# The last attention of an eight-layer block in half-batch sets: scores on four row tiles, one tiled stretch a set

## The reference, cut to what matters

```python
q = _heads(jnp.concatenate([ssm_states, hidden_states], axis=-1) @ Wq, H)      # 32 heads
kcat = jnp.concatenate([rep(ssm_k), rep(k)], axis=2)                           # 8 heads, each for 4 of q
vcat = jnp.concatenate([rep(ssm_v), rep(v)], axis=2)
scores = jnp.einsum('bhqd,bhkd->bhqk', q, k) / np.sqrt(D)
scores = scores + bias                                                         # a slope per head
scores = jnp.where(mask, scores, -jnp.inf)      # the last 64 states, the last 32 tokens
wei = jax.nn.softmax(scores, axis=-1)
o = jnp.einsum('bhqk,bhkd->bhqd', wei, v)
x = x + o.reshape(B, T, HID) @ Wo
```

## Time and profile before

| | |
|---|---|
| three runs | 2078.51, 2068.67, 2076.16 us (median 2076.16) |
| profiled execution, first to last instruction (no other time of it is given) | 2074.5 us |
| PE busy, whole span | 1853.4 us (89%) |
| DVE, ACT, POOL busy | 1266.8, 1026.9, 730.7 us |
| the changed stage | 1707 to 1954 us of the span |

### The profile page before, as it was taken

One profiled execution on the slowest core, in us unless ns is written; L12 is line 12 of the kernel. 1 busy time (PEld: TensorE's weight loads), 2 busy tenths in 40 slices (PEclk: granted clock), 3 DMA queues, 4 the chain that ended last, 5 costly groups with the idle time before them and its releaser, 6 DMA issues. The chain is left out here.

```text
span 2074.5 us, 42486 instructions
## 1 busy us (share of the span) xinstructions
PE 1853.4 (89%) x12207; PEld 1251.6 (60%) x12216; DVE 1266.8 (61%) x4137; ACT 1026.9 (50%) x2698; POOL 730.7 (35%) x707
## 2 busy tenths in 40 slices
PE   7999999998999888878999989969978799999755
PEld 4677777775565566545666766735545557777533
DVE  6666666665777344656343334368979545656698
ACT  5555555553333443312444434348879524444586
POOL 3333333331000202566455555533300106676410
PEclk9999999999999898979999999989999898999998
DMA  8990000000000000253777776510010111211100
GB/s 305 283 274 1 0 0 0 0 1 0 0 0 0 1 1 33 76 197 120 170 162 169 169 155 136 92 59 2 2 64 1 64 43 26 42 39 36 43 18 24
DMA packets 145607, 145.55 MB, mean 70 GB/s; under 512 B 49376, under 2 KB 133568, under 8 KB 145344
## 3 DMA queue, kind: packets, MB, share of 16 engines
q1 hardware_dynamic: 122432, 113.81, 19.5%
q0 software_dynamic: 23040, 30.01, 8.2%
HBM read 137.12 MB, written 66.44 MB: 98 GB/s over the span
## 5 line engine op out<-in xcount | busy, mean ns | idle before, releaser
L1709 POOL DMA_INDIRECT expert_sums<-moe_rows_in,moe_to x128 | 198.2, 1549 | 158.7 <-DMA expert_sums<-moe_rows_in,moe_to 91.9
L1782 PE MATMUL moe_gate<-moe_places,moe_xt 128*128 x512 | 175.3, 465 | 3.4 <-issue 1.9
L3329 DVE CUSTOM_DVE_ANT_0 ctxt<-wa_score,early 128x128 f32<-128x128 f32 x512 | 114.2, 286 | 101.3 <-PE wa_score L3179 101.3
L1975 DVE COPY moe_ht_e<-moe_turned 128x256 f32<-128x256 f32 x128 | 54.4, 425 | 193.9 <-PE moe_turned L1790 192.5
L570 ACT ACTIVATE ga_prob<-ga_score,ga_neg_max 128x128 f32<-128x128 f32 x256 | 99.6, 390 | 125.7 <-DVE ga_neg_max L443 125.7
L3141 POOL TENSOR_TENSOR ctxt<-ctxt,wa_top 128x512 f32<-128x512 f32 x128 | 131.6, 1040 | 75.4 <-DVE wa_top L3329 75.4
L2065 POOL TENSOR_TENSOR ln_rstd<-ln_var,half 128x4 f32<-128x4 f32 (+1 forms) x16 | 21.5, 1346 | 362.1 <-DVE ln_var L2061 362.1
L190 POOL TENSOR_TENSOR ga_q_inv<-ga_q_sum,half 128x4 f32<-128x4 f32 x64 | 64.4, 1007 | 224.3 <-DVE ga_q_sum L426 224.3
L3278 ACT ACTIVATE wa_pt<-wa_turned 128x512 f32<-128x512 f32 x128 | 76.5, 598 | 129.7 <-PE wa_turned L3188 129.7
L325 PE MATMUL ga_summed<-ga_wo,ga_out_t 128*128 128x256 f32 x512 | 121.2, 380 | 0.7 <-ACT ga_out_t L578 0.7
L1782 PEld LDWEIGHTS moe_gate<-moe_places,moe_xt 128*128 128x128 f32 x512 | 90.5, 189 | 47.2 <-issue 12.1
(11 more groups left out here) (491 smaller groups left out, 4777.6 us busy)
## 6 DMA issues: line engine op xcount, KB each, us to landing
moe_places<-in_L_ffn_packed SPq DMA_DIRECT2D x128, 608.0 KB
slot_x<-zeros SPq DMA_DIRECT2D x24, 1076.0 KB, 16.3
moe_rows_in<-slot_x SPq DMA_DIRECT2D x128, 134.5 KB, 3.0
wa_v<-v_ctx SPq DMA_DIRECT2D x16, 180.0 KB, 3.1
early<-in_L_xattn_Wq SPq DMA_DIRECT2D x5, 512.0 KB, 7.8
x<-in_x SPq DMA_DIRECT2D x4, 512.0 KB, 9.6
ga_wo<-in_L_xattn_Wo SPq DMA_DIRECT2D x1, 2048.0 KB, 15.1
expert_sums<-zeros SPq DMA_DIRECT2D x2, 1024.0 KB, 8.4
```

The lines of the kernel that those rows point to most:

```text
L1709: pool.indirect_dma_start(out=mem.sums[j % SUMS], out_offset=bass.IndirectOffsetOnAxis(ap=to[:, j:j + 1], axis=0), in_=y[:, j, :], in_offs ...
L1782: last = pe.matmul(both[j % 2][:, 0:2 * FE], xt[:, j % 2, c, :], packed[:, place, c * 2 * FE:(c + 1) * 2 * FE].rearrange("p a n -> p (a n) ...
L3329: ins = dve.tensor_tensor_reduce(unit[:, x, :], score[k % 3][:, x * P:(x + 1) * P], w.table[:, k, x, :], 1.0, NEVER, ALU.add, ALU.max, top ...
```

## The change

A set is now half a batch: 4 units, each with a bank of its own (`score` has four banks instead of three), so all four groups of heads, on all four row tiles, are scored in one block of 16 matmuls. Right behind it come the two mixes of earlier sets (the second half of set s-2, the first of s-1). Then all work on the whole array stands together: turning or projecting a batch, four units of turns (the last two of set s-1, the first two of set s), turning back set s-2. To make room, the batch's turn and projection share the bank of `turn_back` (`od` is a part of `back`). ACT copies mixes in two halves; DVE's add stands before the fourth unit of an even set; POOL spreads queries once a set, before its four subtractions. The loops, SP's too, are written out, and the semaphores start without credits.

```diff
-        score = [bank(f"score{j}") for j in range(3)]
+        score = [bank(f"score{r}") for r in range(R)]
...
-        mix_t, back, od = bank("mix_t"), bank("back"), bank("od")
+        mix_t, back = bank("mix_t"), bank("back")
+        od = back[:, 0:H]
...
+                def scores(s):
+                    b, u = divmod(s, 2)
+                    if u == 0 and b >= 1:
+                        pe.wait_ge(made.sem, made.at(HC * b - 1))
+                        pe.wait_ge(keyed.sem, keyed.at(2 * b - 1))
+                    behind(pe, biased, s * R - 1)
+                    for x in range(X):
+                        for r in range(R):
...
+                            last = pe.matmul(score[r][:, x * P:(x + 1) * P], w.qd[rows, b % 2, X * u + x, :], w.keys[rows, b % 2, X * u + x, :],
...
+                def turn_probs(n):
+                    pe.wait_ge(lowered.sem, lowered.at(n))
+                    behind(pe, pt_moved, n - 2)
...
+                def tiled(s):
+                    if s < SETS:
+                        scores(s)
+                    if s >= 2:
+                        pe.wait_ge(mt_moved.sem, mt_moved.at(2 * (s - 2)))
+                        mix_up(s - 2, 1)
+                    if 1 <= s <= SETS:
+                        mix_up(s - 1, 0)
+
+                def whole(s):
+                    if s >= 5:
+                        pe.wait_ge(chain.sem, chain.at(2 * (s - 3) + 1))
+                    if turning(s) >= 0:
+                        turn_mixed(turning(s))
+                    if summing(s) >= 0:
+                        go_down(summing(s))
+                    for n in range(s * R - 2, s * R + 2):
+                        if 0 <= n < SETS * R:
+                            turn_probs(n)
+                    if s >= 2:
+                        behind(pe, chain, 2 * (s - 3) + 1)
+                        behind(pe, o_moved, turning(s))
+                        behind(pe, added, summing(s))
+                        turn_back(s - 2)
+
+                for s in range(SETS + 2):
+                    tiled(s)
+                    whole(s)
+                pe.wait_ge(chain.sem, chain.at(2 * (SETS - 1) + 1))
+                go_down(B - 2)
...
+                for s in range(SETS + 2):
+                    if s >= 2:
+                        move_mixed(s - 2, 1, 2 * (s - 1) if s <= SETS else 2 * (s - 2) + 1)
+                    if 1 <= s <= SETS:
+                        move_mixed(s - 1, 0, 2 * (s - 1))
+                    for n in range(s * R - 2, s * R + 2):
+                        if 0 <= n < SETS * R:
+                            exp(n)
+                        if n == s * R - 2 and turning(s) >= 0:
+                            move_out(turning(s))
+                    if s % 2 == 0 and s + 2 < SETS:
+                        move_keys(s // 2 + 1)
```

More of the change, by code:

```diff
@@ L3143, in batch @@
[L3143 to L3162, removed]
+                def spread(b, c):
+                    behind(pool, scored, (2 * b - 3) * R + R - 1)
+                    spread_queries(pool, w, c, w.q[:, c, b * S:(b + 1) * S], b % 2).then_inc(made.sem, 1)
+                def lower(n):
+                    pool.wait_ge(biased.sem, biased.at(n))
+                    unit = low[:, n % LOWS, :, :]
+                    pool.tensor_tensor(unit, unit, top[:, n % LOWS, :].unsqueeze(2).to_broadcast([P, X, P]), ALU.subtract).then_inc(lowered.sem, 1)
@@ L3164, in _ @@
+                for s in range(SETS):
+                    if s + 2 < SETS:
+                        spread(s // 2 + 1, s % 2)
+                    for r in range(R):
+                        lower(s * R + r)
+                    if s == SETS - 3:
+                        norm.root(pool, 0, 0, LASTG)
             @block.tensor
             def _(pe):
[L3166 to L3176, removed]
+                def scores(s):
[5 more added lines that the diff above has]
+                    for x in range(X):
+                        for r in range(R):
@@ L3182, in scores @@
                                 last.then_inc(scored.sem, 1)
[L3184 to L3188, removed]
+                def turn_probs(n):
+                    pe.wait_ge(lowered.sem, lowered.at(n))
+                    behind(pe, pt_moved, n - 2)
+                    for x in range(X):
+                        last = pe.transpose(turned[n % 2][:, x * P:(x + 1) * P], low[:, n % LOWS, x, :], mem.ident[:, :])
@@ L3203, in mix_up, with turn_back @@
                             last = pe.matmul(mix_t[32 * k:32 * k + 32, x * P + kv_half * 64:x * P + kv_half * 64 + 64],
-                                             v[:, j % 2, QUAD * u + x, head * WD1:head * WD1 + 32], columns[:, :, k, :], start=True, stop=True)
+                                             v[:, b % 2, X * u + x, head * WD1:head * WD1 + 32], columns[:, :, k, :], start=True, stop=True)
                     last.then_inc(mixed_s.sem, 1)
[L3207 to L3211, removed]
+                def turn_back(s):
+                    pe.wait_ge(mt_moved.sem, mt_moved.at(2 * s + 1))
+                    for x in range(X):
+                        last = pe.transpose(back[:, x * P:(x + 1) * P], mt[:, s % 2, x, :, :].rearrange("p k n -> p (k n)"), mem.ident[:, :])
@@ L3219, in turn_mixed, with go_down @@
                     last.then_inc(turn_o.sem, 1)
[L3221 to L3222 removed]
+                def go_down(b):
+                    pe.wait_ge(o_moved.sem, o_moved.at(b))
                     for c in range(HC):
[L3224 removed]
+                        last = pe.matmul(od[:, :], ot[:, c, :], w.wo[:, c, :], start=(c == 0), stop=(c == HC - 1))
@@ L3225, in go_down @@
                     last.then_inc(downed.sem, 1)
[L3227 to L3242, removed]
-                        if k == 6:
-                            turn_back(t, j, 0)
-                        if k == 7 and before >= 1:
-                            turn_mixed(t, j - 1)
@@ L3352, in batch @@
-                def batch(t, j, before=2, final=False):
-                    for k in range(U):
-                        if k < U - LEAD:
-                            lower(t, j, k + LEAD)
-                        elif not final:
-                            lower(t, j + 1, k + LEAD - U)
-                        if k == 2 and before >= 2:
-                            add(t, j - 2)
-                        if k == 3 and before >= 1:
-                            normalize(t, j - 1, 1)
-                        if k == 7:
-                            normalize(t, j, 0)
-                        if final and k == 1:
-                            norm.shifts(dve, 0, 0, LASTG)
-                        if final and k == 6:
-                            norm.scales(dve, 0)
-                            norm.lift(dve, 0)
@@ L3370, in _ @@
-                for k in range(LEAD):
-                    lower(0, 0, k)
-                batch(0, 0, before=0)
-                batch(0, 1, before=1)
-                for t in range(1, B // 2 - 1):
-                    batch(t, 0)
-                    batch(t, 1)
-                t = B // 2 - 1
-                dve.wait_ge(stat.sem, stat.at(t, -3))
-                norm.variance(dve, 0, LASTG)
-                batch(t, 0)
-                batch(t, 1, final=True)
+                                              inv[:, :, :].unsqueeze(3).to_broadcast([P, X, 4, WD]), ALU.mult))
@@ L3427, in _ @@
-                sp.wait_ge(placed[0].sem, placed[0].at(t, 16 + 15))
+                read_values(0)
+                read_values(1)
+                for b in range(B - 1):
+                    place(b, 0)
+                    if b + 2 < B:
+                        read_values(b + 2)
+                    place(b, 1)
+                    realign(b)
+                place(B - 1, 0)
+                sp.wait_ge(placed[0].sem, 16 * B)
 class TernaryWeights:
```

284 lines of the change are left out of this document (121 added, 163 removed).

## The result

The changed kernel takes 2011.41 us (median of 4 runs, 2009.22 to 2017.57), the kernel before 2072.41 (4 runs, 2062.22 to 2078.51): a ratio of 0.972 [0.968, 0.975]. The profiled execution took 2009.22 us with a span of 2007.4.

A forecast was written before the change was run, and what follows sets the result against it. TensorE bounds the changed stage (93% busy). Start 21.5, 28 sets x 5.75 = 161, variance 1 and end 18 sum to 201.5 us against 247: 2029.5, said as 2031 us; range 2015 to 2055, the forecast's own 2021 to 2043.

The forecast's parts named there:

- the score block: TensorE's 16 score matmuls of a set on four row tiles: 1.1 us, bounds 1.08 and 2.0.
- the mixes: One TensorE block of 32 matmuls right behind the scores: 1.05 us, bounds 1.0 to 1.25.
- the odd set: TensorE's time for one half-batch set: 5.6 us if odd, 5.9 if even, mean 5.75 against 7.3 before.
- the end: From the stage's last scores to its last statistics: 18 us, against 13.3 before.
- The wait before the third turn: TensorE waits 0.44 us before a set's third turn, until the first exponential frees its bank.
- The fourth turn: TensorE's fourth turn needs the second exponential: waits 0.08 us in an even set, 0.46 in an odd one.
- The start (first three sets) 21.5: The stage's first three sets run at granted clock 0.50, 7.2 us each, 21.5 for three.
- 45 us go: 2074.5 - 45: Changed stage falls from 247 to 201.5 us, so the profiled span of 2074.5 becomes 2029.5.
- A: Rival: four row tiles go two by two in the scores, 25 us given back, 2057; chance 0.09.
- B: Rival: TensorE's clock stays at or falls to its lower level; 2150 for the whole stage; chance 0.05.
- D: Rival: gain lost in waits costed at nothing (POOL, read-back); period 6.8 or more, 2058 to 2074; chance 0.06.
- C: Rival: PE faster than reckoned until POOL binds; 28 x 5.3 and 17 at the start, 2012 to 2020; chance 0.12.

The follow-up runs named there:

- a sixth instruction: Changed kernel with every spreading of the queries done twice on POOL: 2034.87 us, ratio 0.984 [0.981, 0.986].
- the first repeats: Both kernels run again with no edit: the kernel before 2066.89 us, ratio 0.999; the changed one 2019.6 us, ratio 0.976.
- two by two: Changed kernel with a set's 16 score matmuls again on two row tiles at a time: 2035.44 us, ratio 0.984 [0.981, 0.987].

## Why the prediction was right in direction and wrong in time

Right, term by term: the score block (1.11 for 1.1); the mixes (1.03 for 1.05); the odd set 5.55 for 5.6 and the even one 5.97 for 5.9, so 28 sets took 161.75 us (1707.15 to 1868.90) where the sum had 161 and 1 for the variance; the end 18.9 (1868.90 to 1887.78) for 18. The wait before the third turn is there at 0.34 on the engine (0.50 in start to start, for 0.44). The fourth turn loses 0.35 in the odd set and 0.08 in the even one, read as the length of the row's two turns less 0.88 (1.23 and 0.96), for 0.46 and 0.08. The bank, freed by ACT's exponential, is what both wait for, as forecast; where the profile names POOL in even sets, the unit needed had been ready for 1.1 us. The Trainium skill ("TensorE: Matmul & The Clock Gate", Part 3, Measured speedup vs the span model) gave an estimate of 1.15 for the block, from a figure that it measured with 512 moving columns; the trace, with 128, has 1.11 and comes nearer to four tiles fully abreast: the row of 32 records on four tiles takes 1.17, that of 16 on two tiles 1.16.

Wrong, two steps:

1. "The start (first three sets) 21.5": it took 16.5 (1690.61 to 1707.15). I carried the 20 us at 0.50 of the earlier trace rows over to a stage that begins with other blocks. In the changed kernel only 6.8, 6.8 and 3.4 us of the start ran at the lower level in the three executions, in the kernel before 20.5 and 23.9. That is 5 us, and with the other terms' small differences the stage came out at 197.2 for 201.5. How much of the 5 us is the clock is not shown, since no execution of the changed kernel has a start that is all at the lower level: with 6.8, 6.8 and 3.4 us of it, the first three sets took 16.54, 16.67 and 16.47.

2. "45 us go: 2074.5 - 45", made from one execution, and the range with no term for it. In that execution and in the one profiled after, the part that the change does not touch differs by 16.4 us ahead of the stage and 0.8 behind it. Stage and rest together: 4.3 + 16.4 + 0.8 = 21.5 below 2031, 2009.5, which is the 2009.22 of the run. Read against more runs: the kernel before has a median of 2071.19 in the 17 runs beside the first repeats, 5 below the 2076 from which I set out; 2031 - 5 - 4.3 - 0.8 = 2021, and two further sets of runs of the changed kernel gave 2019.6 and 2020.0. The first four, at 2011.4, lie 9 below; the profiled one of them has the earliest start of the stage of all executions, and I take them for a low draw of the same scatter, which no run proves. Measured by 2019.6 and 2020.0, the forecast is 11 us too high, and they lie inside 2015 to 2055; so that the first four fell outside it takes the low draw as well as the two steps. The rows that warned of it were at hand: the runs of before spread over 10 us, and a granted clock of 0.97 means that time at the lower level lies ahead of the stage, and can come and go. Nor do the bounds of the terms add up to the forecast's own range: they give 2019.5 to 2050, not 2021 to 2043, and A comes to 2056, not 2057. 2011 lies outside either way.

Of the rivals, A is refuted by the blocks of 1.11; B by 1.00 through the steady part, also in the variant with the turns in their own set, where TensorE is busy only 81% (84.64 of 105 us from 1760 on; ahead of that one stretch of 3.4 us, at 1735, was at 0.50); D by a period under 6. C's sum (2012 to 2020) came nearest in time for the wrong reason: its start of 17 us was right, but its period of 5.3 with POOL binding was not; POOL binds only with a sixth instruction, at 6.11. The mean period of 5.3 came only when turn_back was moved, and then TensorE bound it.

What stays open: why the start of the stage keeps to the lower clock for a shorter time. The variant with the turns in their own set has a period of 7.3 and yet only 3.4 us of it at the start, and two by two has 10.2, so a shorter period is not the cause; nothing here tells apart what else differs in the first blocks. Open too is what the first sets would cost at the lower level throughout, and whether a few us of the time ahead of the stage are the change's.

## What to carry to other kernels

A forecast made from one profiled execution takes over that execution's clock: look at how the runs scatter, find the stretch whose clock is below 1.00, and put it into the range even where no code there changes. When blocks are joined to save switches, ask what the neighbours of each block were hiding: here all of the gain went when the turns no longer stood half a set behind their scores. And where a joined row of blocks waits for its own bank, put a block from the end of the row into the gap: together with the earlier copy on ACT that was worth 11 us more. Before a wait is put down to the engine that the profile names, look up which unit the waiting instruction needs and when it was ready.

## Unexpected on the hardware

POOL's subtraction has records of 1.04 us, but a full queue of them advances by 1.02 or less (6.11 for six; four turns released 1.0 apart). Matmuls that switch from one pair of row tiles to the other run into one another: 32 records in 1.65 us for two pairs, 1.10 for all four tiles. One switch of array shape cost some 0.15 where a block was split (0.29 for two), against the 0.09 that I had taken from the blocks before.
